# Attention units of a two-layer kernel: the TensorE order of plain scores, the projection and transposed scores

## What is computed

```python
h   = _ln(x, ln1_g, ln1_b) + (silu(t) @ W_ada.T + b_ada)
qkv = (h @ Wqkv.T).reshape(b, n, 3, 16, 64)          # 16 heads of 64
q, k = _ln(q, qn_g, qn_b), _ln(k, kn_g, kn_b)        # per head
scores = einsum('bhnd,bhmd->bhnm', q, k) / sqrt(64)
o = einsum('bhnm,bhmd->bhnd', softmax(scores), v)
x = x + o @ Wout.T
# then: gate, top-k choice of 128 tokens for each of 8 experts, expert MLPs, scatter-add
```

## Time and profile before

| | us |
|---|---|
| median of three runs | 429.25 (429.13 to 431.68) |
| the profiled execution's own time | 428.95 |
| span of its trace | 427.2 |
| units 2 to 28 (95.29 to 323.21) | 227.92 |
| units 29 to 31 (323.21 to 346.69) | 23.48 |

### The profile page before, as it was taken

One profiled execution on the slowest core, in us unless ns is written; L12 is line 12 of the kernel. 1 busy time (PEld: TensorE's weight loads), 2 busy tenths in 40 slices (PEclk: granted clock), 3 DMA queues, 4 the chain that ended last, 5 costly groups with the idle time before them and its releaser, 6 DMA issues.

```text
span 427.2 us, 8341 instructions
## 1 busy us (share of the span) xinstructions
PE 404.1 (95%) x2738; PEld 341.7 (80%) x2738; DVE 273.2 (64%) x648; ACT 284.9 (67%) x532; POOL 193.4 (45%) x203
## 2 busy tenths in 40 slices
PE   6999997899999999999999999999999898789996
PEld 5578767778888888888888888888888687666894
DVE  3665557767666666666666667666765635987733
ACT  3357466578777777777777777777787337768541
POOL 7501317485566657765765667567657000300000
PEclk9999999999999999999999999999999998999999
DMA  6760000290000000000000000000000000000001
GB/s 127 199 145 1 2 2 0 77 364 5 0 3 2 0 2 2 2 0 2 3 2 0 0 0 1 0 0 0 1 0 2 0 2 1 2 2 0 2 2 49
DMA packets 7792, 10.67 MB, mean 25 GB/s; under 512 B 403, under 2 KB 4302, under 8 KB 7758
## 3 DMA queue, kind: packets, MB, share of 16 engines
q1 hardware_dynamic: 6718, 9.73, 8.1%
q10 hardware_dynamic: 1040, 0.52, 0.4%
HBM read 8.68 MB, written 0.52 MB: 22 GB/s over the span
## 4 chain that ended last, share of the span: by engine, by line
PE 82%; DVE 9%; POOL 4%; issue 3%; ACT 2%; DVEq 0%; POOLq 0%; ACTq 0%
PE pair L1488 26%; PE pair L1440 10%; PE pair L1459 8%; PE bank L1478 6%; PE bank L1473 6%; PE pair L1245 5%; PE pair L1712 2%; PE pair L1724 1%; PE pair L1329 1%; PE pair L1405 1%; PE pair L1614 1%; PE bank L1245 1%; POOL rstd L455 1%; PE pair L1669 1%; PE pair L1354 1%
## 5 line engine op out<-in xcount | busy, mean ns | idle before, releaser
L1488 PE MATMUL pair<-v_s,probs_T 128*128 128x129 f32 x1024 | 128.4, 275 | 0.6 <-ACT probs_T L702 0.6
L1488 PEld LDWEIGHTS pair<-v_s,probs_T 128*128 128x128 f32 x1024 | 124.5, 192 | 4.7 <-ACT probs_T L702 0.9
L1016 DVE TENSOR_REDUCE negmax<-pair 128x1 f32<-128x512 f32 x128 | 88.1, 689 | 50.0 <-PE pair L1459 49.8
L702 ACT ACTIVATE probs_T<-bank 128x512 f32<-128x512 f32 x128 | 73.1, 596 | 49.7 <-PE bank L1478 39.5
L500 POOL TENSOR_TENSOR q_s<-kq,k_s 64x512 fp32r<-64x512 f32 x29 | 37.1, 1281 | 78.0 <-DVE k_s L1004 78.0
L1459 PE MATMUL pair<-k_s,q_s 128*128 128x512 f32 x128 | 59.4, 464 | 2.5 <-DVE negmax L1016 2.5
L490 POOL TENSOR_TENSOR qk_rstd<-qk_ms,minus_half 128x8 f32<-128x8 f32 x32 | 53.1, 1660 | 2.6 <-POOL qk_ms L486 0.2
L1473 PE MATMUL bank<-q_s,k_s 128*128 128x512 f32 x128 | 50.8, 397 | 0.0
L1478 PE MATMUL bank<-q_shift,k_low 128*128 128x512 f32 x128 | 50.6, 395 | 0.2 <-DVE q_shift L1023 0.2
L1038 DVE SCALAR_TENSOR_TENSOR x_att<-pair,o_rec,x_att 128x128 f32<-128x128 f32 x128 | 38.5, 344 | 1.1
L500 POOL TENSOR_TENSOR k_low<-kq,k_s 64x512 fp32r<-64x512 f32 x29 | 36.7, 1264 | 2.2
(11 more groups left out here) (292 smaller groups left out, 699.6 us busy)
## 6 DMA issues: line engine op xcount, KB each, us to landing
fc_raw<-in_L_cond_fc2s_dram SPq DMA_DIRECT2D x1, 2048.0 KB, 13.8
x_in<-in_x_dram ACTq DMA_DIRECT2D x1, 512.0 KB, 3.9
w<-in_L_cond_mlp_w_dram SPq DMA_DIRECT2D x2, 256.0 KB, 3.0
wout<-in_L_cond_Wout_dram SPq DMA_DIRECT2D x1, 512.0 KB
k_low<-k_low SPq DMA_DIRECT2D x1, 512.0 KB, 8.4
q_shift<-q_shift SPq DMA_DIRECT2D x1, 512.0 KB, 9.9
b_all<-in_L_cond_b2s_dram SPq DMA_DIRECT2D x1, 512.0 KB, 10.5
out_dram<-final SPq DMA_DIRECT2D x2, 256.0 KB, 2.2
```

What stands on the lines that cost most here:

```text
L702: act.activation(probs_T[:, k % 2, :], bank[2 + k % 2][:, :], ACT.Exp).then_inc(exp_done, 1)
L1016: dve.tensor_reduce(negmax[:, c:c + 1], bank[0][:, :], AX, ALU.max, negate=True).then_inc(max_done, 1)
L1488: last = pe.matmul(pair4[:, c // 2, c % 2 * (D + 1):(c % 2 + 1) * (D + 1)], probs_T[:, k % 2, c * P:c * P + P], v_s[:, r % (2 * PAIRS), k, :],
```

## The change

In each unit's list on PE the plain scores of chunk 1 move from ahead of the projection to between its two groups of three matmuls, and the plain scores of chunk 2 move behind the third transposed scores. `project` takes the halves it shall make; its waits stay with the first half, its increment with the second. No instruction is added or taken away, and the lists of the other engines stay as they are.

```diff
-            def project(p, p_in, head):
-
-                if not (isinstance(p, int) and p in (1, 3)):
+            def project(p, p_in, head, chunks=(0, 1)):
+
+                if 0 in chunks and not (isinstance(p, int) and p in (1, 3)):
...
-                for c in range(2):
+                for c in chunks:
...
-                last.then_inc(qkv_done, 1)
+                if 1 in chunks:
+                    last.then_inc(qkv_done, 1)
...
-                if live:
-                    scores(u, r, 1)
...
                 if due(u, 0, UNITS - 4):
-                    project(u + 3, r + 3, head)
+                    project(u + 3, r + 3, head, (0,))
+                if live:
+                    scores(u, r, 1)
+                if due(u, 0, UNITS - 4):
+                    project(u + 3, r + 3, head, (1,))
+                if back:
+                    scores_T(u - 1, r - 1, 2)
                 if live:
                     scores(u, r, 2)
-                if back:
-                    scores_T(u - 1, r - 1, 2)
```

## The result

The changed kernel takes 423.52 us (median of six, 422.78 to 424.43) beside 429.73 for the kernel before on the same chip (six, 428.68 to 431.68). The ratio is 0.985, with a 95% interval of 0.982 to 0.988: 1.5% faster, where 1.1% was forecast. The medians differ by 6.2 us; 4.9 was forecast, and the lower end of the forecast range, 423.4 from 429.25, allows 5.85. The profiled execution takes 422.88 us with a span of 421.1, 6.1 less than the span before.

What follows compares the result with a forecast made beforehand. PE was taken to set the pace in units 2 to 28; 3.9 us saved there plus 1.0 in units 29 to 31 made 4.9 off 429.25, so 424.3 us, forecast's own range 423.6 to 425.3, 8-in-10 range 423.4 to 427.2.

Steps and rivals of the forecast that it cites:

- What bounds the kernel, and what scores 1's wait costs: Units 2 to 28: PE sets the pace; the wait costs 0.13 us, 0.20 with a new head, together 4.1.
- a second way: Units 2 to 28: unit 15's length without its stall, 8.30 us, charged to all 27 units, saving 3.8 us.
- The new head's register work is hidden: Eight units with a new head: 0.07 us of register work each counted as hidden; otherwise 0.6 us come back.
- Scores 2 release just in time: Units 2 to 28: weight load released 3.10 us after scores 0, free until 3.21, 0.11 us spare, costing nothing.
- DVE and POOL behind it: Units 2 to 28: later row maxima delay nothing; sum of squares at 4.35 us, keys' high part due at 5.10.
- rival 1: Units 2 to 28: the wait moves to scores 2, 1.9 us back, 426.2 us; chance 0.13.
- rival 2: Units 2 to 28: projection can't be issued ahead, 0.07 us shows in every unit, 426.2 us; chance 0.07.
- rival 4: POOL's round trip: later maximum 2 delays the next unit's transposes, each unit 0.2 us longer, 433.7 us; chance 0.05.
- rival 3: Units 2 to 28: all 7.8 us of idle weight loads are on the path, 420.5 us; chance 0.03.
- Units 29 to 31: Third transposed scores fill the hole ahead of scores 2: 0.46 us each in units 30 and 31, 0.1 in 29.
- Behind unit 31 "the same work": What follows unit 31 was taken as the same work, with no difference in the sum.
- "The profiled execution is 0.3 us from the median, so the difference carries over": Whole kernel: 4.9 us off the profiled 428.95 was also taken off the median of 429.25.

Runs made afterwards that it cites:

- Experiment 4: Changed kernel with scores 1 one projection matmul later, behind the fourth instead of the third; median 428.03 us, ratio 0.995 to the kernel before.
- experiment 3: Changed kernel with the third transposed scores back behind scores 2, scores 1 still moved; median 435.18 us, ratio 1.012 to the kernel before.
- experiment 1: Changed kernel with scores 2 ahead of the third transposed scores again in units 29 to 31; median 425.69 us, ratio 0.990 to the kernel before.
- experiment 2: Kernel before with the third transposed scores ahead of scores 2 in units 29 to 31 alone; median 428.75 us, ratio 0.997 to the kernel before.
- experiment 5: Kernel before with the third transposed scores ahead of scores 2 in all units, scores 1 not moved; median 428.31 us, ratio 0.996.
- experiment 6: The changed kernel run again without any edit; median 424.41 us, ratio 0.986 to the kernel before.
- experiment 7: Changed kernel plus four filler transposes behind the last unit's mixes and four behind the last transposes of x; median 424.05 us, ratio 0.986.
- experiment 8: Experiment 7 plus eight filler transposes between the first norm's first two turns and four more ahead of them; median 422.92 us, ratio 0.984.
- experiment 10: Changed kernel with four filler transposes instead of sixteen ahead of the first count in the gate's stage; median 424.02 us, ratio 0.985.

## Why the prediction was right in its mechanism and wrong in size

- *What bounds the kernel, and what scores 1's wait costs*: right. 19 waits at 0.13 and 8 at 0.20 make 4.1 us; 4.12 was measured. I took 3.9, between that and a second way (3.8) that charged unit 15's length without its stall, 8.30 us, to all units; the changed units took 8.289 on average, 0.01 less, which makes 0.3 over 27 units.
- *The new head's register work is hidden*: right, no longer unit for it.
- *Scores 2 release just in time*: right. Release forecast at 3.10, measured at 3.12, which leaves 0.09 of the 0.11 us to the free point that I had worked out (3.21). Experiment 4 moved it by one pitch and paid 0.13 a unit, experiment 3 by two and paid 0.35, as the distance of 1.16 us plus 0.11 says.
- *DVE and POOL behind it*: right to a few hundredths (sum of squares at 4.37 for 4.35, high part at 5.09 for 5.10). Rivals 1, 2 and 4 didn't come.
- *The weight loads' idle time as a price (rival 3)*: wrong. 7.8 us of it were removed in units 2 to 28 for 4.12 us, and experiment 4 shows the same 7.8 for 3.57. That idle weight loads are lost time one for one was my own step. Lateness has to be counted from the matmul that the load would start with: 0.24 us in unit 15 before (206.28 for 206.04), and the loads are idle for 0.05 more because a load of 0.19 us doesn't fill a pitch even without a wait. Of the 0.24 some 0.11 are free and 0.13 are paid.
- *Units 29 to 31*: 1.0 forecast, 1.16 measured. Units 30 and 31 gave 0.46 each as worked out. Unit 29 gave 0.24 and not 0.1: I compared weight load with weight load, but the old load ran a pitch ahead of its matmuls (load at 326.37, transposes from 326.60), and the new one starts with them (322.11). The mixes started 3.82 us after scores 0 before and start at 3.58 now.
- *Behind unit 31 "the same work"*: this is the step that failed. The sum puts that stage at no difference. The work is the same, its time isn't: 0.75 us less in the profiled pair, because the clock fell there before and not after. The profile before showed the fall (a granted clock of 0.57 from 357 to 361 us, and the fillers in the chain with 0.20 us each, for 0.12 in the changed kernel), and I had read the stage as a constant. Among the profiles with sixteen fillers the stage takes 80.3 to 80.5 us where the clock fell in it and 79.8 where it didn't. The forecast from the profile is 4.9, the profiled difference 6.1: 0.22 and 0.16 from the two terms above, 0.07 ahead of unit 2, 0.75 from this.
- *"The profiled execution is 0.3 us from the median, so the difference carries over"*: the same fault in the step from the profile to the median. Beside the experiments the kernel before was timed 54 times. 31 of these have a mean granted clock of 0.992 or less, where its profiled execution has 0.994; none of the twelve of the changed kernel has. So the median before holds more time at the lower clock than its profile did. Nine of the 54 have 0.997 or 0.998 and take 428.2 to 429.1 us; five of the twelve have 0.998 or more and take 422.8 to 423.3. Between their middle values lie 5.75 us, between the shortest of each 5.4. Units 2 to 31 and the start give 5.35 of it by the profiles.

What is shown: the two gains, their places and sizes, and their independence. Experiments 1 to 5 account for 5.3 of the 6.1 us. What stays open is why the clock falls in the gate's stage in some kernels and executions and not in others. With sixteen fillers it fell there in all three profiles with the old last units (the kernel before, experiments 1 and 3) and in none of the seven with the new ones (the changed kernel, experiments 2 and 4 to 8). So the order of the last units seems to have a part. It doesn't decide alone: the kernel before has executions with a mean clock of 0.998, and in experiment 10 the clock fell with the new last units and four fillers. For this term, then, the forecast's miss is partly chance: the one profile that it started from had the fall.

## What to carry to other kernels

Where one PSUM bank is refilled after a reduction, look for the shortest time from the matmul that fills it to the weight load of the next. Here it was 1.16 us where the matmul's own load had been in time, and 1.26 from scores 0, which stand behind the mixes. Count the matmuls between two of them: six pitches of 0.232 us were enough, four or five were not, and moving one of them without its neighbour made the kernel 1.2% slower. Price a stall by the spacing of matmul starts, not by idle weight loads, and compare start with start. Read the granted clock of every stretch before taking an untouched stage for a constant, and the mean clocks of the other executions before carrying a profile over to a median.

## What was unexpected of the hardware

- Weight loads idle for 0.29 us ahead of scores 1 or scores 2 (a load 0.24 us late) cost 0.13 us; idle for 0.52 us (0.49 late) they cost 0.35. A load 0.02 late cost nothing.
- At the start the clock fell to its lower level for about 3.5 us in the profile of experiment 6, after gaps of 0.8 and 1.2 us on PE, and unit 2 started 1.65 us later. The same gaps stand in the changed kernel's first profile without a fall. By their lengths and mean clocks seven of its twelve executions had one. With twelve filler transposes in those gaps none of six had a mean clock below 0.998.
- Four fillers instead of sixteen ahead of the counts didn't shorten the stage in the kernel before: the clock stayed low for some 7 us instead of 3.5, and the stage took 80.49 us for 80.51.
